# One attention and expert block on one core: heads gathered by DMA, gates turned on TensorE, maxima cast by ScalarE, another order of steps

## The reference

```
Q, K = rope(x @ qw), rope(x @ kw);  V = x @ vw          # 16 heads of 8
score = Q K^T / sqrt(8), causal;  weights = softmax(score)
x = layernorm(x + (weights V merged) @ ow)
probs = softmax(x @ router_w + router_b); gates = the 2 largest of 4, scaled to sum 1
h_e = silu(x @ w1_e) * (x @ w3_e);  out = sum_e gates_e * (h_e @ w2_e)
return layernorm(x + out)
```

## Time and profile before

| | us |
|---|---|
| median of 3 runs | 412.04 |
| lowest and highest | 410.81 and 413.67 |
| profiled execution | 413.73 |
| its span, first to last instruction | 412.0 |
| busy in the span: TensorE, VectorE, ScalarE, GpSimd | 386.8, 310.0, 260.8, 208.2 |

### The profile page before, as it was taken

One profiled execution on the slowest core, in us unless ns is written; L12 is line 12 of the kernel. 1 busy time (PEld: TensorE's weight loads), 2 busy tenths in 40 slices (PEclk: granted clock), 3 DMA queues, 4 the chain that ended last, 5 costly groups with the idle time before them and its releaser, 6 DMA issues.

```text
span 412.0 us, 7446 instructions
## 1 busy us (share of the span) xinstructions
PE 386.8 (94%) x2402; PEld 203.3 (49%) x2424; DVE 310.0 (75%) x1022; ACT 260.8 (63%) x373; POOL 208.2 (51%) x274
## 2 busy tenths in 40 slices
PE   6897979999999999999999998999999999999992
PEld 2441232323323233232332434888888888888780
DVE  2869799899999999999999761455586568656653
ACT  1361527686866868668686687666566756666560
POOL 7177478542614436044360422756476546755662
PEclk9996889999999999999999999999999999999997
DMA  7474011375232232322310000000000000000000
GB/s 233 160 216 95 0 22 29 88 237 173 55 94 45 47 82 55 95 45 46 85 27 3 3 1 2 0 2 1 2 1 25 2 1 27 2 0 2 25 2 25
DMA packets 46164, 21.14 MB, mean 51 GB/s; under 512 B 30379, under 2 KB 44331, under 8 KB 46126
## 3 DMA queue, kind: packets, MB, share of 16 engines
q1 hardware_dynamic: 42718, 18.44, 17.1%
q10 hardware_dynamic: 3408, 2.23, 1.8%
HBM read 13.11 MB, written 7.35 MB: 50 GB/s over the span
## 4 chain that ended last, share of the span: by engine, by line
PE 80%; DVE 10%; ACT 3%; issue 3%; DMA 2%; POOL 1%; POOLq 0%; SPq 0%; ACTq 0%; DVEq 0%
PE o_bank L1264 16%; PE bank L1338 11%; PE t_bank L1338 11%; PE bank L1223 10%; PE t_bank L1351 10%; PE t_bank L1246 8%; PE small_bank L1223 5%; DVE maxima L960 2%; DVE x_w L956 2%; PE o_bank L1360 2%; PE t_bank L1176 2%; ACT num L766 1%; DVE mg_w L956 1%; DMA wqk<-in_kw 1%; DVE mg_t L956 1%
## 5 line engine op out<-in xcount | busy, mean ns | idle before, releaser
L766 ACT ACTIVATE num<-t_bank 128x1024 f32<-128x1024 f32 (+2 forms) x160 | 141.9, 940 | 65.3 <-PE t_bank L1246 65.2
L659 POOL TENSOR_TENSOR hid_lo<-num,q_op 128x512 fp32r<-128x512 f32 x63 | 81.8, 1302 | 57.7 <-ACT q_op L830 56.5
L621 POOL TENSOR_SCALAR_AFFINE_SELECT num<-num 128x512 f32<-128x512 f32 x64 | 40.2, 638 | 102.2 <-ACT num L766 101.9
L1264 PE MATMUL o_bank<-num,v_op 128*32 128x512 f32 (+3 forms) x768 | 80.1, 497 | 0.1
L1223 PE MATMUL bank<-k_op,q_op 128*128 128x512 bf16 (+7 forms) x241 | 65.3, 327 | 3.4 <-DVE maxima L956 1.3
L830 ACT ACTIVATE q_op<-num 128x512 fp32r<-128x512 f32 x64 | 40.5, 632 | 42.6 <-DVE num L1104 42.1
L960 DVE TENSOR_REDUCE maxima<-bank 128x1 f32<-128x512 f32 x83 | 55.3, 684 | 2.0 <-PE bank L1223 0.8
L1246 PE MATMUL t_bank<-q_op,k_op 64*128 64x512 bf16 (+3 forms) x384 | 49.4, 334 | 3.7 <-ACT num L766 1.3
L1104 DVE TENSOR_TENSOR num<-bank,num 128x512 f32<-128x512 f32 x32 | 22.1, 691 | 34.3 <-ACT num L837 34.0
L1223 PEld LDWEIGHTS bank<-k_op,q_op 128*128 128x128 bf16 x257 | 20.7, 98 | 53.9 <-DVE maxima L960 21.8
L1104 DVE TENSOR_TENSOR num<-t_bank,num 128x512 f32<-128x512 f32 x32 | 22.1, 690 | 26.3 <-ACT num L837 24.0
(11 more groups left out here) (162 smaller groups left out, 654.6 us busy)
## 6 DMA issues: line engine op xcount, KB each, us to landing
q_op<-q_scratch SPq DMA_DIRECT2D x64, 48.0 KB
w_raw<-in_w_all SPq DMA_DIRECT2D x6, 512.0 KB, 4.0
k_op<-k_scratch SPq DMA_DIRECT2D x28, 96.0 KB, 2.2
xT<-in_x_feat SPq DMA_DIRECT2D x4, 256.0 KB, 6.0
x_res<-in_x_tok ACTq DMA_DIRECT2D x4, 256.0 KB, 3.1
q_scratch<-num SPq DMA_DIRECT2D x2, 384.0 KB, 2.8
k_scratch<-num SPq DMA_DIRECT2D x2, 384.0 KB, 2.9
out_tokens<-num SPq DMA_DIRECT2D x3, 256.0 KB, 2.3
```

The costliest lines, as they stand in the source:

```text
L621: pool.affine_select(out=tile, in_=tile, compare_op=ALU.is_ge, fill=0.0, base=0, pattern=[[0, GH], [1, P]], channel_multiplier=-1)\
L659: pool.tensor_tensor(hid_lo[:, m % HB, :], hid[:, m % HB, :], hid_hi[:, m % HB, :].bitcast(F32), ALU.subtract).then_inc(f_lo, 1)
L766: act.activation(num[:, t % PB, :, off:CH].rearrange("p (k i) t -> p i k t", i=2)[:, :, h:h + each, :], t_bank[k % TB][:, :, 0:each * (CH ...
L1264: ins = pe.matmul(o_bank[h * QD:(h + 1) * QD, off:CH], v_op[w][:, kt, h, :], num[:, t % PB, h, off:CH], start=kt == 0, stop=kt == TI * (c ...
```

## The change

- **NORM is gone.** V has eight 1s a head instead of one, so that `o_bank` holds each denominator in eight rows. ScalarE copies `o_bank` into `o_sb[g % 2]` (one for both chunks). SP sends it by 8 DMAs a group (`gather_heads`, 8 rows of 4 KB each) to `o_all` (which is xT's space) and `den_all`, one stage later. `between` r = 0 is now a reciprocal and a multiply over 128x512 on VectorE, and r = 1 multiplies the result by `wo`; copies and transposes ahead of it go.
- **The rows of maxima are cast by ScalarE**, which counts `rows_cast`; TensorE waits for a ring slot by both counts (`slot_free`).
- **`STEADY_ORDER` and `FIRST_ORDER`** are new, without n, and with the m's elsewhere.
- **Gates are turned.** r = 13 makes the gates of a chunk, at r = 14 TensorE turns them (16 rows of 128), VectorE copies them, SP stores them to DRAM and loads each expert's row into all partitions (`spread_gates`). When an expert is complete VectorE multiplies its bank by these rows and adds it to `sum_t`, which starts from x1 (turned). Only the sum is turned back, once a chunk (`TR_STEP`, n = 19), and statistics and normalisation read PSUM.
- **`between` starts at n = 3** (`NEXT_AT`) and has 16 steps.
- **Prologue.** The Q weight and half of x's first chunk are on SP's queue, the K weight and the other half on ScalarE's. TensorE waits for each weight and each turned copy by itself, and warms up with one more product. VectorE does the sums of turns of n = 2 and 3 and the third part of n = 2. SP issues all key loads; the cast of the identity is awaited only by the first MROWS. Group 1's chunk 1 is loaded after the first rows are sent.
- **End.** VectorE normalises the last tile alone, from PSUM, in halves.

```
-STEADY_ORDER = "ssmttssspssttsspssttsspsstspsttssspmsttsssptsspssttssspssttsspssttsspsnttnpp"
-FIRST_ORDER = "ssssmssssnsssststsstsstsssttsspssttsspmsttssspssttsspssttsspssnttppp"
+STEADY_ORDER = "sssmttssspsttssspssttsspstsstspssttsspssttsspmstsstsspssttsspsssttpssttppp"
+FIRST_ORDER = "ssssmsssssssststsstsstsssttsspssttsspmsttssspssttsspssttsspssttppp"
@@ steps
-TR_STEP = Y_STEP = EO_STEP + 1
-STAT_STEP = Y_STEP + UNITS - FT + 1
+TR_STEP = EO_STEP + UNITS - FT + 1
+STAT_STEP = TR_STEP + 1
+NEXT_AT = E_LAST
+def next_steps(n, i):
+    r = n - NEXT_AT
+    return [(i + 1 + r // UNITS, r % UNITS)] if i + 1 + r // UNITS < CHUNKS else []
@@ SP
+            sp.dma_start(wqk[:, 0, :], qw).then_inc(ld_proj[0], 16)
+            sp.dma_start(xT[0:P // 2, 0:CH], x_feat[0:P // 2, 0:CH]).then_inc(ld_x[0], 16)
...
-                sp.wait_ge(job_read, SB + JOB[s, step] + 1)
+                sp.wait_ge(rows_cast, rows_until(JOB[s, step]) + 1)
...
+            def gather_heads(n):
+                b, g = divmod(n, NG)
+                sp.wait_ge(o_copied, 1 + NC * (n + 1))
+                for h in range(GH):
+                    for k, dst in enumerate((o_all, den_all)):
+                        at, rows = g * QD + h * DH, h * QD + k * DH
+                        sp.dma_start(dst[at:at + DH, b * S:(b + 1) * S], o_sb[n % 2][rows:rows + DH, :])\
+                            .then_inc(heads_in[b][n % 2], 16)
...
                         sp.dma_start(w_raw[:, :], w_all[:, bass.ds(n * PIECE, PIECE)]).then_inc(ld_w, 16)
+                        if n > 0:
+                            gather_heads(n - 1)
...
+            def spread_gates(ch):
+                sp.wait_ge(g_copied, ch + 1)
+                sp.dma_start(g_dram[ch, :, :].rearrange("e (t p) -> (e t) p", p=P), gates_t[:, :]).then_inc(g_stored, 16)
+                sp.wait_ge(g_stored, 16 * (ch + 1))
+                for e in range(E):
+                    sp.dma_start(gate_rows[ch % 2][:, e, :], g_dram[ch, e, :].partition_broadcast(P))\
+                        .then_inc(g_loaded[ch % 2][e], 16)
+                if ch == 0:
+                    gather_heads(GROUPS - 1)
@@ ScalarE
+                    if step[0] == "MROWS":
+                        _, c, use = step
+                        act.wait_ge(job_ready, JOB[n + 1, step] + 1)
+                        act.activation(max_rows[c][:, :], ring(n + 1, step)[0:NPR * PARTS * NB, 0:P], ACT.Copy)\
+                            .then_inc(rows_cast, 1)
...
-                    act.wait_ge(f_tr, ch * E + e + 1)
-                    for half in halves(ch, e):
-                        act.activation(eo_sb[:, e % 2, half], bank[4 + e % 2][:, half], ACT.Copy).then_inc(f_eo, 1)
@@ VectorE
+                if r == 0:
+                    b, at = ch // NC, slice(ch * CH, (ch + 1) * CH)
+                    for i in range(2):
+                        dve.wait_ge(heads_in[b][i], 16 * GH * NG)
                     dve.wait_ge(c_y, 1 + ch)
+                    dve.reciprocal(den_all[:, at], den_all[:, at]).then_inc(c_mg, 1)
+                    dve.wait_ge(c_mg, ch + 1)
+                    dve.tensor_tensor(mg_t[:, :], o_all[:, at], den_all[:, at], ALU.mult).then_inc(c_mgs, 1)
...
+                if n >= EO_STEP and (n - EO_STEP) % FT == 0 and n < EO_STEP + UNITS:
+                    e = (n - EO_STEP) // FT
+                    dve.wait_ge(g_loaded[ch % 2][e], 16 * (ch // 2 + 1))
+                    dve.wait_ge(f_w2, ch * UNITS + FT * (e + 1) + HB)
+                    for k, half in enumerate(halves(ch, e)):
+                        dve.tensor_tensor(gated[:, e % 2, half], bank[4 + e % 2][:, half], gate_rows[ch % 2][:, e, half],
+                                          ALU.mult).then_inc(f_eo, 1)
...
+                        dve.tensor_tensor(sum_t[:, half], gated[:, e % 2, half], (sum_t if e else x1_tw)[:, half],
+                                          ALU.add).then_inc(f_y, 1)
@@ TensorE
+                def slot_free(s, step):
+                    earlier = SB if s < GROUPS else 1
+                    if JOB[s, step] >= earlier:
+                        earlier = JOB[s, step] - earlier + 1
+                        pe.wait_ge(job_read, scores_until(earlier))
+                        if JOBS[earlier - 1][1][0] == "MROWS":
+                            pe.wait_ge(rows_cast, rows_until(earlier))
...
+                if r == 14:
+                    pe.wait_ge(c_done, 1 + 2 * ch + 2)
+                    pe.wait_ge(rows_cast, rows_until(NJOBS))
+                    pe.transpose(bank[7][0:E * TI, 0:P], gates[:, :, :].rearrange("p e t -> p (e t)"), ident[:, :])\
+                        .then_inc(g_turned, 1)
+                if r == 1:
+                    pe.wait_ge(c_mgs, ch + 1)
```

More of the change, by code:

```diff
@@ L510, in _ @@
                     .then_inc(out_stored, 16)
+            for s in range(1, GROUPS + 1):
+                stage(STAGES[s], s, s % 2, load=s < GROUPS - 1)
+            for ch in range(0, CHUNKS):
+                spread_gates(ch)
+                if ch == 0:
+                    continue
+                store_out(ch - 1)
+            store_out(CHUNKS - 1)
             sp.wait_ge(out_stored, 16 * (CHUNKS + 1) + 16)
@@ L675, in _ @@
                 experts(0, n)
+                for step in next_steps(n, 0):
+                    between(*step)
             for i in range(0, CHUNKS - 1):
@@ L680, in _ @@
                     experts(i, n)
-                    between(i + 1, n - HEAD)
+                    for step in next_steps(n, i):
+                        between(*step)
             for n in range(HEAD, Z_STEP + 1):
@@ L932, in _, with stage @@
             third_part(1)
-            for n in range(2, PROJ_FIRST):
-                turns_of(n)
-                if n > 2:
-                    first_rest(n - 1)
-            first_rest(PROJ_FIRST - 1)
-            def stage(plan, s, chain):
+            turns_of(2)
+            sum_of_turns(2)
+            turns_of(3)
+            first_rest(2)
+            sum_of_turns(3)
+            third_part(2)
+            first_rest(3)
+            def stage(plan, s):
                 seen, done = set(), 0
@@ L991, in stage @@
                         experts(0, step[1])
-            CHAIN_0, CHAIN = 0, NC
-            base = steps[0]
-            stage(PROLOGUE, 0, base)
-            for s in range(1, GROUPS):
-                stage(STAGES[s], s, base + CHAIN_0 + (s - 1) * CHAIN)
-            last_base = base + CHAIN_0 + (GROUPS - 1) * CHAIN
+            for s in range(GROUPS):
+                stage(STAGES[s], s)
             def statistics(src, step_sem):
@@ L1137, in experts @@
                     dve.wait_ge(f_rstd, ch + 1)
-                    normalise(lambda i: y_sb[:, i, :], lambda i: z_sb[:, i, :], f_z,
-                              TI // 2 if ch == CHUNKS - 1 else TI)
+                    for k, half in enumerate(halves(ch, E - 1)):
+                        normalise(lambda i: bank[6 + k][:, i * D:(i + 1) * D], lambda i: z_sb[:, i, :], f_z,
+                                  y_mv, y_rstd, range(half.start // P, half.stop // P))
             dve.wait_ge(ld_small, 16 * 6)
             dve.wait_ge(ld_res, 16 * CHUNKS)
-            stage(LAST, GROUPS, last_base)
+            stage(LAST, GROUPS)
             for n in range(E_LAST, HEAD):
                 experts(0, n)
+                for step in next_steps(n, 0):
+                    between(*step)
             for i in range(0, CHUNKS - 1):
@@ L1366, in _ @@
             stage(LAST, GROUPS, 0, 0)
+            pe.wait_ge(rows_cast, rows_until(NJOBS))
             for n in range(E_LAST, HEAD):
                 experts(0, n)
-            pe.wait_ge(job_read, SB + NJOBS)
+                for step in next_steps(n, 0):
+                    between(*step)
             for i in range(0, CHUNKS - 1):
```

340 lines of the change are left out of this document (130 added, 210 removed).

## The result

| | before | changed |
|---|---|---|
| median, us | 412.86 | 439.28 |
| lowest to highest | 410.81 to 413.83 | 434.12 to 440.78 |
| profiled execution / its span | 413.73 / 412.0 | 440.78 / 437.4 |

The ratio is 1.057 (95% interval 1.046 to 1.068): slower, where 403.6 us and a range of 390 to 411 stood. It leaves out 440.78 (the profiled execution) and 440.71, over 1.5% above the fastest of this kernel, so it is not the quotient of the medians.

A forecast was written before the change was run, and what follows sets the result against it. TensorE was taken to bound both long parts, with VectorE leading only from 34.90 to 62.00 us. Gains of 19.6 us against losses of 11.2 made 8.4 us less: 403.6 us at the median, range 390 to 411.

The forecast's parts named there:

- Start to 79.6 us: Prologue and first attention stretch: first score 2.0 us earlier, 5.1 us gained in all, bounds 2.5 to 7.
- Six steady stages: Repeated attention stages, 25.65 us each: transposes leave TensorE, 1.3 us gained per stage, 7.8 in all.
- the hole: 6.2 us without issues in SP's queue in a steady stage, where eight gather issues of 2.4 to 3.4 us would fit.
- the ring: Slots for rows of maxima in attention: ScalarE's cast could delay the third job behind it; nothing was counted.
- The last stage: Last attention stage: two transpose rounds go, reciprocal and multiply make TensorE lose 0.9 us; net 0.3 us gained.
- The reciprocal: VectorE's 128x512 instruction, 3.2 us; TensorE waits at the output projection in three expert chunks, 7.6 us lost.
- Clock: Experts: TensorE's stops at the output projection lower the clock; 3.0 us lost for three stops, bounds 0 and 15.6.
- The gating: Experts: multiply by gate rows and add on VectorE use up a bank's slack at three steps a chunk; 0.6 us lost.
- The gates' way through DRAM: Experts: store and four loads of gates lie inside 10.4 us of cover; without it, the rest of some 7 us per chunk.
- the end: After the last products: two normalisations move from GpSimd to VectorE, one wait less; 0.4 us gained.
- rival 2: Steady stages: the new order or the slot held for ScalarE's cast takes the gain away; 411 us, chance 0.12.
- Rival 3: Experts: stops at the output projection let the clock fall longer, reciprocal 4.3 us; 8.6 us slower, 421 us, chance 0.08.

The follow-up runs named there:

- second measurement: The changed kernel measured again, unaltered, with its own trace of an execution of 435.55 us: 435.18 us, ratio 1.054.
- Experiment 1: Changed kernel with the eight gathers moved behind the stage's last loads in SyncE's queue: 459.32 us, ratio 1.116.
- Experiment 5: Changed kernel with the eight gathers moved into SyncE's gap, behind the loads that end at 134.2: 436.57 us (1.057), then 434.75 us (1.050).
- Run 4: Changed kernel with the next chunk's steps started one expert step later, at the fourth instead of the third: 434.0 us, ratio 1.052.
- Run 6: Changed kernel with the residual sum written back into its PSUM bank, statistics and normalisation reading it there: 434.14 us, ratio 1.047.
- Run 8: Changed kernel with gathers in the gap, reciprocal in pieces, next chunk's steps one later, residual and gated output kept in PSUM: 413.18 us, ratio 1.001.
- run 12: Run 8 with chunk 0's reciprocal in pieces in two attention stages and the summed output's turn one expert step later: 409.28 us, ratio 0.989.

## Why the prediction was wrong

**Start to 79.6 us** (5.1 gained): nearly right, a little high. The first score comes 3.3 us earlier (21.04 against 24.33), where 2.0 stood; the first copy of `o_bank` 4.3 us (45.4 against 49.7), the next pair 4.9 and 3.5. In the second measurement the copies come 3.8, 4.4 and 3.0 earlier.

**Six steady stages** (7.8 gained): wrong. The step that failed is "at the 0.30 to 0.43 of these two an issue 2.4 to 3.4 us are filled, and nearly double would fit". I priced an SBUF-to-SBUF gather by the issues that happened to stand around the hole. They took 0.62 to 0.70, 5.4 us in all; that fits the hole of 6.2 too, but the new order had changed what stands behind it. My own sentence, that the rows would be that much late, was the outcome. From the first stage's second copy to the sixth's, changed needs 129.1 us (82.97 to 212.07) and the kernel before 128.2 (86.51 to 214.73): five stages without any gain: the first is 2.1 us longer, the other four 1.2 shorter together. With the gathers in the gap a stage is 24.94, not 24.3: the rest is 0.5 us for the split of the maxima on GpSimd and small waits at the scores, which I had not counted since TensorE showed only 0.2 us of them before. Experiments 1 and 5 show the queue's part; that ScalarE's cast costs the ring nothing is only suggested by the stage of 24.94.

**The last stage** (0.3 gained): wrong. TensorE waited 1.9 us for the multiply, not 0.9, the granted clock of the stretch is 0.92 in place of 1.00, and the last steady stage, which lies in it too, brought no gain; it is 3.3 us longer. In the second measurement the wait is the same, the clock 0.96, and the stretch 2.1 longer.

**The reciprocal** (3.2 us; TensorE waits 2.8, 2.4 and 2.4): right. It took 3.34 four times, and the waits were 3.2, 1.8 and 1.8, 6.8 in place of 7.6. The estimate of 4.3 us from the Trainium skill, VectorE: DVE Perf Modes, "First, the fixed hardware budget", is not borne out by the trace: 3.34 us are 6.5 ns an element with the fixed part in it. Taking it out gave 9.5 to 10.7 us with what follows, where 7.6, 0.9 in the last stage and the clock's 3.0 stood for it.

**Clock** (3.0 lost): too low for the first trace (6.8), right for the second (3.4). TensorE was to be busy 6 us less in the experts and was 3.5 longer in the first trace, 0.9 in the second. Of these 9.5 and 6.9 us the lower level is 6.8 and 3.4; the rest, 2.7 and 3.5, stands beside some twenty stops, the first product behind a stop taking 0.50 in place of 0.39 us. I had counted three stops.

**The gating** ("at three steps a chunk it is used up by some tenths: 0.6 lost, bounds 0 and 2.5"): this is the step that decided the case. I looked at what a gating costs, 1.4 us in place of 1.1, and not at the steps on which it, and everything else of the next chunk, now fell. The change moved the chunk's steps from the seventh expert step to the third. The gating, which fell on r = 0, 4, 8 and 12 before, now falls on r = 3, 7, 11 and 15, beside the variance, x1's low part and the choice of experts, and x1's normalisation beside three of GpSimd's subtractions in a row. The five waits behind that are 18.7 us, a term my sum did not have. Runs 4, 6, 8 and 12 each moved one or two of its causes and the waits followed; in run 12 there are 4.4 us left. The rule of the Trainium skill that I quoted for the adds (SBUF — State Buffer, "Who interferes with whom"), and which would have named the normalisation too had I read on to scalar instructions, I gave the mean of one row. The kernel before shows the same slow form, four tiles of the output's normalisation in 2.82 us at 343.80; it cost nothing there, since nothing waited in the step behind it.

**The gates' way through DRAM** (hidden) and **the end** (0.4): right; no wait for gate rows shows, the loads landed in 3.8 us, and from the last product's start to the last instruction it is 8.5 us in place of 9.3.

Of the rivals, 2 had the outcome for the steady stages, no gain, but not the cause: the gathers in SyncE's queue, not the new order or ScalarE's cast, for which at most the 0.6 us between 24.94 and 24.3 are left. Rival 3 had the sign, but by another mechanism: its long stops at the projection did not come, they had my own forecast's size. The slower case that came, a chain of VectorE's steps each a little too long for the step of TensorE beside it, was not among them.

What stays open: why a stop is followed by the lower level in one execution and not in the next, which is the 3 us between the two traces in the experts; and how the 18.7 us divide between the new places of the steps and the gating by rows, since no run has the one without the other.

## What to carry to other kernels

When one engine's side work is shifted against another's steps, add up that engine's work for each single step and hold it against the step's length; VectorE's share of 62% over the experts said nothing here, where one step had some 4 us of work (product, gating, addition, four normalisations, from 318.6 to 322.3 us in changed) for the 2.1 that TensorE needs. A long instruction in an in-order queue is cheap in pieces spread over light steps and dear in one place (3.34 us whole: 6.8 us of waits; four of 0.94 in the experts: none, but two in each of two attention stages: 0.8 and 1.6 us). A DMA is priced by its own kind of issue, and by what stands behind it in its queue until the next thing that someone waits for.

## What the runs showed of the hardware

- A reciprocal of fp32 takes 3.34 us for 128x512 and 0.94 us for 128x128, with 0.25 us for 16 elements: 6.1 to 6.3 ns an element over a fixed 0.15.
- An issue on SyncE took 0.43 us for a load of weights, 0.62 to 0.71 for a gather of 32 KB from SBUF to SBUF, 0.71 to 0.75 for the zero rows and for rows of maxima.
- A VectorE scalar instruction of 128x128 from SBUF to SBUF took 333 ns alone and up to 1307 ns beside GpSimd; from PSUM 395 to 411, with GpSimd's subtractions beside it or not.
- After a stop of 2.46 us TensorE's matmuls ran at the lower clock level for about 3.5 us, from 328.8 to 332.3; after one of 1.79 us, at 313.3, they did not. The same stop of the same kernel can go either way: of four stops of 2.44 to 2.46 us in the two traces of changed two were followed by the lower level, and one of 1.25 us was in the first trace (287.2) and not in the second (285.3).
